# A Mamba-2 block on one core: rows of decays repeated by transfers through a DRAM scratch instead of by selector products

## What is computed

```python
def _mamba2(x, Win, convw, convb, dtb, Alog, Dsk, normw, Wout):
    zxbcdt = x @ Win                                  # 256 -> 512 + 640 + 8
    z, xBC, dt = jnp.split(zxbcdt, ...)
    xBC = silu(causal depthwise conv of width 4 (xBC) + convb)
    xs, Bm, Cm = jnp.split(xBC, ...)                  # 8 heads x 64, state 64
    dt = jax.nn.softplus(dt + dtb); A = -jnp.exp(Alog); dA = jnp.exp(dt * A)
    # scan over tokens, per head:
    #   h = dA_t * h + dt_t * B_t x_t ;  y = C_t h
    y = y + Dsk * xs;  y = y * silu(z)
    y = y * rsqrt(mean(y * y) + 1e-5) * normw
    return y @ Wout
x = x + concat(mamba2_f(norm(x)), flip(mamba2_b(flip(norm(x))))) @ Wo + bo
x = x + ffn(norm(x))
```

## Time and profile before

| | |
|---|---|
| median of 3 runs | 683.64 us |
| the profiled execution | 683.62 us, of which the span from the first to the last instruction is 681.8 us |
| PE busy | 650.2 us, 95% of the span |
| DVE busy | 517.7 us, 76% |
| ACT busy | 480.1 us, 70% |
| POOL busy | 388.0 us, 57% |
| granted clock of TensorE | 0.995 of full speed |
| DMA | 24.04 MB, mean 35 GB/s |

### The profile page before, as it was taken

How to read it: one execution, slowest core, us unless ns; L and a number is a source line. 1 busy time by engine, 2 the same in 40 slices (tenths; PEclk the granted TensorE clock), 3 DMA queues, 4 the chain that set the end, 5 groups by cost and what they waited for, 6 DMA issues and landing times.

```text
span 681.8 us, 13628 instructions
## 1 busy us (share of the span) xinstructions
PE 650.2 (95%) x4236; PEld 514.6 (75%) x4236; DVE 517.7 (76%) x1053; ACT 480.1 (70%) x1126; POOL 388.0 (57%) x467
## 2 busy tenths in 40 slices
PE   1699999999999999999999999999999999999996
PEld 1478778787788878887788877888687877888784
DVE  4769686986869779696769868697796968789453
ACT  4477867587875967769676787759677596766832
POOL 5035646577366754865465772757538664557833
PEclk9999999999999999999999999999999999999997
DMA  7310201012010211003010120101210020101100
GB/s 211 135 24 2 86 2 24 1 48 70 0 23 0 70 45 23 0 8 95 13 23 0 46 69 0 23 0 62 54 23 0 0 85 1 24 2 47 39 1 31
DMA packets 21561, 24.04 MB, mean 35 GB/s; under 512 B 3936, under 2 KB 17312, under 8 KB 21536
## 3 DMA queue, kind: packets, MB, share of 16 engines
q1 hardware_dynamic: 21536, 23.73, 12.1%
HBM read 13.24 MB, written 4.19 MB: 26 GB/s over the span
## 4 chain that ended last, share of the span: by engine, by line
PE 90%; DVE 5%; ACT 2%; issue 2%; POOL 1%; DVEq 0%; POOLq 0%
PE mi L536 16%; PE pj L393 10%; PE pj L395 10%; PE pj L394 9%; PE py L502 9%; PE py L514 7%; PE sbk L450 4%; PE mi L486 4%; PE mi L591 4%; PE mi L466 4%; PE sbk L447 2%; PE mi L522 2%; DVE xc L1255 1%; PE mi L457 1%; PE gm L473 1%
## 5 line engine op out<-in xcount | busy, mean ns | idle before, releaser
L1255 DVE SCALAR_TENSOR_TENSOR xc<-pj,cw,xc 128x511 f32<-128x511 f32 (+2 forms) x240 | 177.8, 741 | 33.9 <-ACT xc L847 31.0
L879 ACT ACTIVATE lx<-sbk,neg_s 128x128 f32<-128x128 f32 x512 | 141.6, 374 | 69.7 <-PE sbk L450 62.1
L393 PE MATMUL pj<-xnt_hi,w_hi 128*128 128x512 f32 x288 | 123.8, 430 | 9.1 <-DVE xc L1255 5.9
L1735 POOL TENSOR_TENSOR yg<-yg,sz 128x512 f32<-128x512 f32 x60 | 76.8, 1285 | 85.2 <-DVE yg L1305 85.2
L395 PE MATMUL pj<-xnt_hi,w_lo 128*128 128x512 f32 x288 | 114.3, 397 | 0.0
L394 PE MATMUL pj<-xnt_lo,w_hi 128*128 128x512 f32 x288 | 114.1, 396 | 0.0
L536 PE MATMUL mi<-wc,yg 128*128 128x256 f32 x480 | 113.9, 383 | 0.0
L536 PEld LDWEIGHTS mi<-wc,yg 128*128 128x128 f32 x480 | 88.1, 190 | 13.3 <-issue 2.3
L1267 DVE TENSOR_TENSOR xdt<-mi,dt 128x512 f32<-128x512 f32 x64 | 42.6, 686 | 61.1 <-PE mi L466 61.1
L1283 DVE TENSOR_TENSOR mx<-lx,gm 128x512 f32<-128x512 f32 x128 | 85.7, 681 | 2.3
L1743 POOL TENSOR_TENSOR sqsum<-sqsum,sq 128x512 f32<-128x512 f32 x45 | 57.6, 1281 | 48.9 <-ACT sq L898 48.2
(11 more groups left out here) (168 smaller groups left out, 1149.8 us busy)
## 6 DMA issues: line engine op xcount, KB each, us to landing
xin<-in_x SPq DMA_DIRECT2D x8, 512.0 KB, 3.6
cc<-bcm SPq DMA_DIRECT2D x32, 128.0 KB, 2.3
xres<-in_x SPq DMA_DIRECT2D x8, 512.0 KB, 3.5
out<-ot SPq DMA_DIRECT2D x32, 128.0 KB, 1.7
cz<-bcm SPq DMA_DIRECT2D x16, 128.0 KB, 2.4
yg<-in_fwin SPq DMA_DIRECT2D x2, 576.0 KB, 6.3
xs<-in_bwin SPq DMA_DIRECT2D x1, 576.0 KB, 4.6
sz<-in_bwin SPq DMA_DIRECT2D x1, 576.0 KB, 5.6
```

Of the source, the lines that this page charges most:

```text
L393: pe.matmul(ps[:], hi(k), xnt_hi[:, k, :], start=(k == 0), stop=False)
L879: i = nc.scalar.activation(lx[:, n % 2, Q * c:Q * c + Q], sbk[bank][:, Q * c:Q * c + Q], ACT.Exp, bias=neg_s[:, d, o:o + 1])
L1255: i = dve.scalar_tensor_tensor(xc[:, t, to], pj[bank][:, of], cw[:, d, t, KW - 1 - s:KW - s], xc[:, t, to], ALU.mult, ALU.add)
L1735: pool.tensor_tensor(yg[:, d, p, :], yg[:, d, p, :], sz[:, d, p, :], ALU.mult).then_inc(yg_ready, 1)
```

## The change

- Instead of the three bf16 pieces, s itself is transposed in fp32: one transpose a scan with (chunk, head) on 32 partitions. ACT copies it to `s_rows` (`row_copy`) and takes its exponential (`row_decays`). SP writes both to a DRAM scratch `rows_dram` (four DMAs each: `put_rows`, `put_decays`) and reads them back repeated over the partitions: a pair of heads in one DMA of 128 partitions x 4 KB (`repeat_heads`), exp(s) of a pair in two DMAs of 64 partitions x 1.5 KB (`repeat_decays`). POOL's `piece`, `remainder` and `selectors`, PE's twelve `spread` products a scan, `sel`, `selp`, `st_bf` and the banks `sbk` go.
- The bias of 32768 went with the pieces, so the exponent is bounded instead: for even heads ACT computes relu(s_u - s_t) (four 128-column activations) and then exp of minus that; for odd heads POOL computes min(s_t - s_u, 0) (four 128-column tensor_scalar) and ACT then exp. `decay` is one 512-column activation a head. The product with `gm` is as before; entries that may not be seen are zero in `gm`.
- exp(s_t) for the state term comes ready from the scratch; ACT's `es` activations go.
- All of it is done in place: `bs` (8 heads x 512) takes the place of `lx` and `mx`, `es` (4 pairs) that of `es` and `c2`. A pair's slot is loaded again when the `inter` of that pair in the scan before is done (`pair_done` on SP).
- The two freed PSUM banks become a third `pj` and a second `py`.
- The order of the instructions on each engine is another one. On ACT, `decay_w` (exp) of a reversed scan now stands ahead of `gate(b, 1, 8)` (silu), and `row_decays` of the next forward scan (exp) stands between `gate(nxt, 0, 5)` and `conv_end(nxt, 0, 2)` (both silu).

```diff
-        pj, sbk, py, mi = banks("pj", 2), banks("sbk", 2), banks("py", 1), banks("mi", 2)
+        pj, py, mi = banks("pj", 3), banks("py", 2), banks("mi", 2)
...
-        lx = sb("lx", [P, 2, T])
-        mx = sb("mx", [P, 4, T])
-        es = sb("es", [P, 2, T])
-        c2 = sb("c2", [P, 2, T])
+        s_rows = sb("s_rows", [NCH, 2, 2, Q])
+        bs = sb("bs", [P, NH, T])
+        es = sb("es", [P, KI, T])
...
+            def put_rows(phase, it, b, d):
+                bank, used = misc_use(phase, it, f"{d}ST")
+                sp.wait_ge(mi_free[bank], used + 2)
+                alone(sp)
+                for c in range(NC):
+                    sp.dma_start(rows_dram[d, 0, :, Q * c:Q * c + Q], s_rows[NH * c:NH * c + NH, d, 0, :]).then_inc(rows_stored, 16)
...
+            def pair_done(b, d, p):
+                if not (isinstance(b, int) and b == d == 0):
+                    bank, used = py_use(b - 1 + d, 1 - d, p)
+                    sp.wait_ge(py_full[bank], used + 1)
+                    alone(sp)
+
+            def repeat_heads(b, d, p):
+                if p == 0:
+                    sp.wait_ge(rows_stored, 16 * NC * (2 * b + d + 1))
+                    alone(sp)
+                pair_done(b, d, p)
+                sp.dma_start(bs[:, 2 * p:2 * p + 2, :], rows_dram[d, 0, 2 * p:2 * p + 2, :].partition_broadcast(P)).then_inc(bs_loaded[p], 16)
+
+            def repeat_decays(b, d, p):
...
+                for e2 in range(2):
+                    sp.dma_start(es[HP * e2:HP * e2 + HP, p, LATER[d]],
+                                 rows_dram[d, 1, 2 * p + e2, LATER[d]].partition_broadcast(HP)).then_inc(es_loaded[p], 16)
...
             def turn(it, more):
                 if more:
                     load_x("loop", it, it + 2)
+                put_rows("loop", it, it + 1, 0)
                 copy_c(it + 1, 0)
+                put_decays(it + 1, 0)
+                repeat_heads(it + 1, 0, 0)
+                repeat_decays(it + 1, 0, 0)
+                repeat_decays(it + 1, 0, 1)
+                repeat_heads(it + 1, 0, 1)
...
             def s_transposed(phase, it, b, d):
-                pe.wait_ge(piece_ready[PIECES - 1], 2 * b + d + 1)
+                released(phase, it, f"{d}S")
                 ps, full = misc(phase, it, f"{d}ST")
                 alone(pe)
-                pb = ps[:, 0:T // 2].bitcast(BF16)
-                for c in range(NC):
-                    mm = pe.transpose(pb[:, Q * c:Q * c + Q], spc[:, c, :], identb[:])
-                mm.then_inc(full, 1)
-
-            def spread(b, d, name):
...
+                pe.transpose(ps[0:NCH, 0:Q], s_all[:, d, 0].rearrange("p c h -> p (c h)"), ident).then_inc(full, 1)
...
+            def row_copy(phase, it, d):
                 ps, free = misc(phase, it, f"{d}ST")
-                nc.scalar.activation(st_bf[0:SROWS, d, :], ps[0:SROWS, 0:T // 2].bitcast(BF16), ACT.Copy).then_inc(free, 1)
+                nc.scalar.activation(s_rows[:, d, 0, :], ps[0:NCH, 0:Q], ACT.Copy).then_inc(free, 1)
+
+            def row_decays(phase, it, d):
...
+                nc.scalar.activation(s_rows[:, d, 1, :], s_rows[:, d, 0, :], ACT.Exp).then_inc(decays_ready, 1)
...
+            def bound(b, d, h):
...
+                act.wait_ge(bs_loaded[h // 2], 16 * (u + 1))
+                for c in range(NC):
+                    o = c * NH + h
+                    i = nc.scalar.activation(bs[:, h, Q * c:Q * c + Q], bs[:, h, Q * c:Q * c + Q], ACT.Relu,
+                                             bias=s_all[:, d, 0, c, h:h + 1], scale=-1.0)
+                i.then_inc(bounded[0], 1)
+
+            def decay(b, d, h):
+                act.wait_ge(bounded[h % 2], KI * (2 * b + d) + h // 2 + 1)
+                nc.scalar.activation(bs[:, h, :], bs[:, h, :], ACT.Exp, scale=1.0 if h % 2 else -1.0).then_inc(decayed, 1)
...
                 if h == 0:
                     dve.wait_ge(gm_ready, u + 1)
-                bank, used = sb_use(b, d, f"h{h}")
-                dve.wait_ge(sb_free[bank], used + 2)
-                dve.tensor_tensor(mx[:, h % 4, :], lx[:, h % 2, :], gm[:], ALU.mult).then_inc(m_ready, 1)
+                dve.wait_ge(decayed, NH * u + h + 1)
+                dve.tensor_tensor(bs[:, h, :], bs[:, h, :], gm[:], ALU.mult).then_inc(m_ready, 1)
...
+            def bound(b, d, h):
...
+                pool.wait_ge(bs_loaded[h // 2], 16 * (u + 1))
+                alone(pool)
+                for c in range(NC):
+                    o = c * NH + h
+                    i = pool.tensor_scalar(bs[:, h, Q * c:Q * c + Q], bs[:, h, Q * c:Q * c + Q], neg_s[:, d, o:o + 1], 0.0, ALU.add, ALU.min)
+                i.then_inc(bounded[1], 1)
+
             def decayed_c(b, d, p):
...
+                pool.wait_ge(es_loaded[p], 32 * (2 * b + d + 1))
+                pool.tensor_tensor(es[:, p, LATER[d]], cc[:, d, LATER[d]], es[:, p, LATER[d]], ALU.mult).then_inc(c2_ready, 1)
```

In the set-up, ACT's `row_copy` and `row_decays` of the first scan stand ahead of its five `conv_end`, and SP's `put_rows` stands behind `copy_c`:

```diff
             conv_start(0, 0, 4)
+            row_copy("start", 0, 0)
+            row_decays("start", 0, 0)
             conv_ends(0, 0, 0, 1, 2)
             conv_ends(0, 0, 3, 4)
             gates(0, 0, 5, 6, 7)
-            act.wait_ge(sel_step, 2)
```

More of the change, by code:

```diff
@@ L328, in _ @@
             copy_c(0, 1)
+            put_rows("start", 0, 0, 1)
+            repeat_heads(0, 1, 0)
+            put_decays(0, 1)
+            repeat_decays(0, 1, 0)
+            repeat_heads(0, 1, 1)
+            repeat_decays(0, 1, 1)
+            repeat_heads(0, 1, 2)
+            repeat_decays(0, 1, 2)
+            repeat_heads(0, 1, 3)
+            repeat_decays(0, 1, 3)
             def turn(it, more):
@@ L659, in reversed_scan @@
                     project(nxt, 0, 7)
+                if not more:
+                    last_sums(b, 0)
             def forward_scan(phase, it, b, last):
@@ L982, in reversed_scan @@
                 if more:
+                    conv_end(nxt, 0, 0)
+                    conv_end(nxt, 0, 1)
+                    gate(nxt, 0, 5)
                     square(phase, it, b, 1, 0)
+                    conv_start(nxt, 0, 4)
+                    row_copy(phase, it, 0)
+                    row_decays(phase, it, 0)
                 if not more:
@@ L1036, in forward_scan @@
-                spread(b, 0, "h6")
-                spread(b, 0, "h7")
+                decay(b, 0, 3)
                 conv_start(b, 1, 2)
+                bound(b, 0, 4)
+                if not more:
+                    fold(4)
+                decay(b, 0, 4)
+                decay(b, 0, 5)
+                if not more:
+                    fold(5)
+                bound(b, 0, 6)
+                decay(b, 0, 6)
+                conv_start(b, 1, 3)
+                decay(b, 0, 7)
                 if more:
@@ L1040, in forward_scan @@
                     norm2_scale(b - 1, 0)
-                if not more:
-                    fold(4)
+                    norm2_scale(b - 1, 1)
+                row_copy(phase, it, 1)
+                row_decays(phase, it, 1)
                 if more:
-                    norm2_scale(b - 1, 1)
-                s_pieces(phase, it, 1)
-                if more:
+                    norm2_scale(b - 1, 2)
                     norm2(phase, it, 0)
                     norm2(phase, it, 1)
-                conv_start(b, 1, 3)
+                square(phase, it, b, 0, 0)
@@ L1409, in reversed_scan @@
                     soft_abs(phase, it)
-                    conv(nxt, 0, 1, 2)
-                outputs(b, 1, 0)
-                mix(phase, it, b, 0, 0)
+                weights(phase, it, b, 1, 1)
+                squares(phase, it, 0)
+                if more:
+                    conv(nxt, 0, 1, 1)
+                    soft_one(nxt)
+                    soft_du(nxt)
+                state(phase, it, b, 1, 2)
+                if more:
+                    soft_dd(nxt)
+                    conv(nxt, 0, 1, 2)
@@ L1435, in reversed_scan @@
+                weights(phase, it, b, 1, 7)
+                if more:
+                    conv(nxt, 0, 3, 3)
+                    conv(nxt, 0, 4, 1)
+                outputs(b, 1, 2)
                 if not more:
@@ L1551, in forward_scan @@
                     feed(phase, it, last, 3)
-                if not more:
-                    fold_ffn()
+                outputs(b, 0, 3)
             setup()
@@ L1798, in forward_scan @@
                 decayed_x(phase, it, b, 0, 1)
+                if more:
+                    mean_square(phase, it, 1)
+                bound(b, 0, 1)
                 decayed_x(phase, it, b, 0, 2)
```

614 lines of the change are left out of this document (250 added, 364 removed).

## The result

The changed kernel takes 693.08 us (median of four runs, 691.73 to 693.18) beside 683.79 for the kernel before: ratio 1.0126, 95% interval 1.0105 to 1.0148. It is slower by 1.3%, where 655 us with a range of 644 to 681 had been forecast. The profiled execution took 691.73 us, its span is 689.8, 8.0 longer than the 681.8 of before.

What follows compares the result with a forecast made beforehand. PE was taken to bound the loop, busy 79.17 of 79.8 us a pass. 683.6 - 29.4 (seven passes, 4.2 each) + 2 (set-up) - 1.5 (last scan) = 654.7, said as 655 us, range 644 to 681.

Steps and rivals of the forecast that it cites:

- POOL's price: Loop: 32 new tensor_scalar a pass at 0.33 us each, 10.6 us; POOL goes from 48.1 to 56.4 us.
- only near the high end: POOL in the loop: at 1.0 us a tensor_scalar POOL is busy 78 us a pass and becomes the bound.
- the tail: Last scan: 2.4 us less on PE and small steps in which nothing changes, -1.5 us.
- the sum: Whole kernel: 683.6 - 29.4 for seven passes + 2 for the set-up - 1.5 for the last scan = 654.7 us.
- 1.0 us for all new waits: Loop: allowance for new waits at PE, so a pass gives 4.2 us instead of 5.2.
- The late rows: Rival, first bound of each scan: ACT and POOL wait for loads of bs; 700 us at 10 us landing; chance 0.12.
- PE's 5.2 us a pass: Loop: removed products less two returning fp32 transposes shorten PE's queue by 5.2 us a pass.
- all of it arrives: Rival, loop: PE stays full and the full gain of 36.4 us comes, 646 us; chance 0.12.
- the set-up: Ahead of the loop: conv_ends some 6 us later, first relu near 50 us; +2 us, between -1 and +6.
- ACT: Loop: ACT gets +2.1 us a pass, 58.9 to 61.0, with ten table loads at 1.29 us and relus at 0.26.
- the ACT rival: Reversed scan: ACT becomes the bound, scan stays near 39.3 us (some 41 with drain); 669 us in all; chance 0.2.
- The rows: Forward scan: s through DRAM takes 9.8 us, landing 3.6; ACT's cover is 9.1, first relu waits within 1 us.

Runs made afterwards that it cites:

- the probes: Ten single POOL instructions, each twice, added to the changed kernel's set-up where POOL is otherwise idle: 693.73 us.
- cheap bound: Changed kernel with POOL's four instructions a head as multiply by 1.0 and add 0.0, leaving out subtraction and bound of odd heads: 650.32 us.
- either version: Reversed scan's gate(b, 1, 8) put ahead of decay_w: in the changed kernel 703.72 us; with cheap subtraction and new set-up 656.33 against 656.00 us.
- the versions with the cheap subtraction: Changed kernel, odd heads: one 512-column broadcast subtraction on POOL, one 512-column relu on ACT: 659.02 us first; with another set-up order 656.00 us.
- the version with the new set-up: Against the 659.02 us version: in the set-up row_copy stands behind the first three conv_ends, row_decays behind the last gate: 656.00 us.
- the last experiment: Against the 656.00 us version: in the loop row_decays behind the forward scan's gates, SP's load of the first heads ahead of put_decays: 675.19 us.

## Why the prediction was wrong, point by point

**The failed step is POOL's price.** "I take 0.33, since kind and length match": 0.725 was measured. 32 x (0.725 - 0.33) = 12.6 us a pass; 56.4 + 12.6 = 69.0, and the pass shows 68.15. The range of the row had been right (0.21 to 1.0), and so had the sentence that POOL is the bound "only near the high end": at 0.725 it is 69 of some 75 over the pass, and that was near enough to take the gain. The choice between the ends was made by the kind of instruction and its columns; the probes show that the pair of operations decides. Run near the price that was taken (0.299), the kernel needs 650.3 us, within the range given and 4 to 5 from the forecast. That it comes so near is in part luck: the passes give 36.9 us there instead of 29.4, and the tail, taken at -1.5, costs 3.1.

**The price of a nearly full POOL was never made a rival.** In the sum it stood as a busy share over the pass (75%), with 1.0 us for all new waits. The earlier trace rows had the warning: POOL was busy 27.0 of 40.3 us in the forward scan and 21.0 of 39.5 in the reversed one. Sixteen bounds come on each and some 1.1 us go: at 0.33 the forward scan has 31.2 of 37.6, at 0.725 it has 37.5 of 37.6, no room at all. The late rows, the rival that ended slower, named the right queue (`decayed_x` and `state` behind a `bound`) for the wrong reason.

**PE's 5.2 us a pass: right.** With a cheap bound the pass gives 5.25. So the allowance of 1.0 us for new waits was too large, and in that run the rival "all of it arrives" is what happens, at 650.3 where it had 646; the rest is the set-up and the tail.

**ACT: right but for small sizes.** Ten table loads a pass (78 in all), each 1.283 us:

```profile
319.75 1.28 ACT L878 ACT_TABLE_LOAD   x1
321.05 0.23 ACT L878 ACTIVATE w_end<-wd 128x32 f32<-128x32 f32 x1
...
321.82 1.28 ACT L874 ACT_TABLE_LOAD   x1
323.11 0.60 ACT L874 ACTIVATE sz<-pj 128x512 f32<-128x512 f32 x1
```

The next activation starts 1.29 to 1.30 us after the load starts, so the drain of about 1380 ns that the Trainium skill, "ScalarE: Activation LUTs", section on what ACT_TABLE_LOAD costs, adds to each switch doesn't show in the changed kernel either. (The 41 us that the ACT rival gives for the reversed scan with that drain don't follow from its terms: 38.6 and the same 6 us of waits are 44.6. Nothing else was built on it.) A relu read from SBUF takes 0.31 us instead of 0.26 (80.2 us for 256, line L890); for 32 of them that is 1.6 us, enough for the 62.2 against 61.0. The ACT rival (0.2) is not what bounded the kernel: with the cheap bound it runs at 650.3 with the same work on ACT, and two loads less changed nothing for the better in either version.

**The rows: in time, with landings longer than taken.** DMA issues: count, KB each, median us to landing.

```profile
bs<-rows_dram SPq DMA_DIRECT2D x64, 512.0 KB, 5.6
es<-rows_dram SPq DMA_DIRECT2D x128, 96.0 KB, 4.7
```

5.6 instead of the 3.6 of `xin` in the earlier trace rows, and the share of the engines is 0.35 (0.4 expected). The cover held for it: 0.7 us of waiting on ACT in all.

**The set-up: right in size (+2.7, +2 taken), and in its way.** The first relu starts at 48.60 ("near 50"):

```profile
48.60 1.28 ACT L890 ACTIVATE bs<-bs,s_all 128x128 f32<-128x128 f32 x4 [0.70 <-DMA bs<-rows_dram]
```

The first product with h0 comes at 58.47, 7.1 us later than the 51.35 of the earlier trace rows; most of it is made up before the reversed scan.

**The tail: wrong in sign, +3.1 instead of -1.5.** "A tail of small steps in which nothing changes" overlooked that PE has waits to lose there and a clock. PE in the last scan of the changed kernel, and the same product of `wc` in the kernel before:

```profile
648.31 1.05 PE L557 MATMUL mi<-cst,sqsum 128*128 128x1 f32 x8 [2.27 <-POOL sqsum L1723]
650.38 3.65 PE L571 MATMUL mi<-wc,yg 128*128 128x256 f32 x8 [1.01 <-DVE hst L1306]
```
```profile
645.21 1.89 PE L536 MATMUL mi<-wc,yg 128*128 128x256 f32 x8
```

PE idles 3.3 us, first for a `sqsum` that stands on POOL behind a bound of 2.8 us, and then runs eight products in 3.65 us that took 1.89 before: the granted clock of 644 to 653 is 0.86, and 1.00 in the same stretch of before. Waits and clock make 5.0 us. Only six "h" and three "p" products of the last scan lie behind the row from which the tail is counted, so 1.9 come back, which leaves the +3.1; a further wait of 0.9 us for POOL's `es` and a last stretch that is 0.9 us shorter nearly cancel. The price of the bound is not all of it: with the cheap bound these two waits are 1.75 us together, but the clock from 604.3 to 613 is 0.73 and the tail is 45.8 us as well. The tails of the versions with the cheap subtraction were 43.3 and, with the other set-up, 45.7. Nor is the clock fixed by the waits: behind waits of 0.6 and 1.1 us the same eight products take 3.75 us in the version with the new set-up and 1.97 in the last experiment. What fixes the clock of this stretch was not told apart.

**One for one with the sum:** -29.4 became +2.2, +2 became +2.7, -1.5 became +3.1.

## What to carry to other kernels

Price a new instruction from a row with the same operations, not only the same kind and size; if there is none and the range of its price reaches the point where its engine fills a stage, that end is a rival with a chance of its own. Compare the added work with the free time of the fullest stage of that engine, not with its share of a pass. And where work is moved from the bound engine to a neighbour, look at what is queued behind it there: the same two table loads were worth nothing in one version, and taking them out cost 10.6 us in another, where it moved the work of the full engine.

## What the hardware showed that was not expected

- A POOL tensor_scalar on 128 columns costs 0.29 to 0.30 us for multiply and add, 0.53 for a minimum or an add alone, 0.64 to 0.65 for both, 0.725 with a column of scalars as operand. One 512-column two-input add with a broadcast operand (1.05) does the subtraction of four of these (2.9 us with their minimum, for which ACT then needs a relu).
- Reading a row of 4 KB repeated over 128 partitions from DRAM lands in 5.6 us at the median, for the bytes for which a plain load took 3.6 before the change; with the added traffic the plain `xin` load itself has a median of 5.2 now, so much of this may be the company and not the repetition; the equally large `xres` load stayed at 3.6 (3.5 before). The two were not separated.
- In the set-up of the changed kernel PE idled 4.65 us for ACT's gates, and in the stretch from 40 to 46 us its granted clock is 0.50, the 1.2 GHz level; before, it was 1.00 there, with PE busy 5.85 of the 6 us.

```profile
41.66 0.79 PE L446 MATMUL pj<-xnt_hi,w_hi 128*128 128x512 f32 x1 [4.65 <-ACT sz L874]
...
40.00:46.00 6.00, 4.34 (x14) 3.65 (x15) 2.33 (x2) 5.21 (x10) 0.00 (x0) 0.50 0.32 71
```

Matmuls of 512 columns start 0.43 us apart there instead of 0.23. The kernel before has the same near its end: behind an idle time of 3.74 us its clock is 0.50 from 671.8 to 677 us. After shorter idle times it goes either way. Four traces have PE idle for 2.5 us for DVE's convolution, ending between 28 and 30 us. Behind it the clock stays 1.00 to 36 us in the kernel before and in the first version with the cheap subtraction; it is 0.50 from 32 to 36 us in the changed kernel and 0.54 from 28 to 34 us in the version with the new set-up. So an idle time of the bound engine can cost more than its length; what decides after a short one is not shown.
